# Differential attention with a dense eight-expert feed-forward: the q/k RMS norm cut into 512-column pieces, and the guard of the first expert weights set earlier

## The reference, cut to what matters

```
q, k, v = x @ wq.T, x @ wk.T, x @ wv.T              # 8 heads of 256
q1, q2  = rms_norm(first half of q), rms_norm(second half)   # halves of 128; k1, k2 likewise
y       = softmax(causal q1 k1) v - lambda * softmax(causal q2 k2) v
x1      = layernorm(x + 0.2 * (y @ wo.T))
w       = softmax over the top 2 of 8 gate logits x1 @ gate, scattered to 8 columns
out     = sum over all experts e of ((silu(x1 @ wi_0[e]) * (x1 @ wi_1[e])) * w[e]) @ wo[e]
result  = layernorm(x1 + out)
```

## Time and profile before

| | |
|---|---|
| runs shown | 9087.93 and 9921.32 us, median 9504.62 |
| the profiled execution, its own time | 9131.31 us |
| its span (core 2, the slowest) | 9129.8 us |
| spans of the eight cores | 9017.3 to 9129.8 us |
| PE busy, DVE busy, ACT busy | 7343.8 (80%), 1951.4 (21%), 2306.1 (25%) us |
| attention stage with projections | 0 to about 2707 us |
| output projection, layer norm, gate | to about 3237 us |
| experts | from 3244.6 us to the end |

### The profile page before, as it was taken

One profiled execution on the slowest core, in us unless ns is written; L12 is line 12 of the kernel. 1 busy time (PEld: TensorE's weight loads), 2 busy tenths in 40 slices (PEclk: granted clock), 3 DMA queues, 4 the chain that ended last, 5 costly groups with the idle time before them and its releaser, 6 DMA issues.

```text
span 9129.8 us, 78951 instructions; the slowest of 8 cores (9017.3 to 9129.8 us)
## 1 busy us (share of the span) xinstructions
PE 7343.8 (80%) x32250; PEld 3269.1 (36%) x32866; DVE 1951.4 (21%) x2548; ACT 2306.1 (25%) x2553; POOL 924.2 (10%) x822
## 2 busy tenths in 40 slices
PE   4546646646649189999999999969999999999996
PEld 2223213313314034444444444424444444444342
DVE  1222221222222511111111111131111111111113
ACT  3565565575560120110110100111001001011011
POOL 0000000000000011111111111101111111111110
PEclk8767767767769589999999999989999999999888
DMA  4001001101103067787787777757777778767664
GB/s 61 5 10 14 10 5 14 14 0 14 14 10 93 0 65 70 72 76 70 70 79 70 70 75 74 70 79 70 76 72 74 72 69 81 69 67 72 63 62 69
DMA packets 1663572, 483.60 MB, mean 53 GB/s; under 512 B 1589097, under 2 KB 1655017, under 8 KB 1661170
## 3 DMA queue, kind: packets, MB, share of 16 engines
q0 software_dynamic: 1655712, 444.71, 49.2%
q1 hardware_dynamic: 7506, 33.80, 1.0%
HBM read 906.34 MB, written 16.78 MB: 101 GB/s over the span
## 4 chain that ended last, share of the span: by engine, by line
PE 70%; ACT 11%; DMA 7%; issue 6%; DVE 5%; another core or an unknown queue 1%; DVEq 0%; POOL 0%; ACTq 0%; SPq 0%; POOLq 0%
PE PB L994 15%; PE P L931 10%; PE PB L925 10%; PE P L925 10%; PE PB L931 10%; DMA WOS<-wom 5%; PE PB L284 4%; ACT ATT L496 4%; PE PB L514 3%; ACT L496 3%; PE PB L609 2%; PE P L508 2%; PE PB L318 1%; PE PB L451 1%; DMA WI1S<-wi 1%
## 5 line engine op out<-in xcount | busy, mean ns | idle before, releaser
L994 PE MATMUL PB<-H,WOS 128*128 128x512 bf16 x8030 | 1850.9, 389 | 181.5 <-DVE H L964 88.3
L947 ACT ACT_TABLE_LOAD x256 | 328.4, 1283 | 4885.5 <-PE PB L931 3382.1
L994 PEld LDWEIGHTS PB<-H,WOS 128*128 128x128 bf16 x8192 | 804.2, 100 | 1228.3 <-issue 382.7
L451 PE MATMUL PB<-QT,KT 128*128 128x512 bf16 (+3 forms) x640 | 299.0, 486 | 865.9 <-ACT ATT L496 739.6
L925 PE MATMUL PB<-X1T,WI0S 128*128 128x512 bf16 x4014 | 919.8, 385 | 13.4 <-DMA WI1S<-wi 8.7
L931 PE MATMUL P<-X1T,WI1S 128*128 128x512 bf16 x4014 | 919.5, 385 | 4.7
L925 PE MATMUL P<-X1T,WI0S 128*128 128x512 bf16 x4013 | 917.9, 385 | 5.8 <-DMA WI1S<-wi 1.2
L931 PE MATMUL PB<-X1T,WI1S 128*128 128x512 bf16 x4012 | 915.9, 384 | 4.7
L496 ACT ACT_TABLE_LOAD x640 | 821.1, 1283 | 291.3 <-PE PB L451 223.6
L911 POOL DMA_DIRECT2D WI0S<-wi x256 | 293.1, 1145 | 3305.9 <-PE PB L931 1643.7
L1009 DVE TENSOR_TENSOR ACC<-ACC,PB 128x512 f32<-128x512 f32 x448 | 308.1, 688 | 1407.9 <-PE PB L994 1407.9
(11 more groups left out here) (125 smaller groups left out, 4241.1 us busy)
## 6 DMA issues: line engine op xcount, KB each, us to landing
WI0S<-wi POOLq DMA_DIRECT2D x256, 512.0 KB, 6.4
WI1S<-wi POOLq DMA_DIRECT2D x256, 512.0 KB, 8.3
WOS<-wom POOLq DMA_DIRECT2D x256, 512.0 KB, 6.4
OXF<-xt SPq DMA_DIRECT2D x16, 1024.0 KB, 6.1
outT<-OUTS SPq DMA_DIRECT2D x32, 512.0 KB, 2.6
XT<-xt POOLq DMA_DIRECT2D x16, 512.0 KB, 29.1
WS<-wqT POOLq DMA_DIRECT2D x8, 1024.0 KB, 9.7
WS<-wkT POOLq DMA_DIRECT2D x8, 1024.0 KB, 9.6
```

The lines of the kernel that those rows point to most:

```text
L451: _t.out = PT.inc(t.matmul(PB[bn][:, qs:512], KT[:, m * T + kt * 128: m * T + (kt + 1) * 128], QT[:, m * T + qb * 512 + qs: m * T + (qb + ...
L947: i = PS.inc(s.activation(SILU[:, c * 512:(c + 1) * 512], h0p[par][c][1], AF.Silu))
L994: mm = t.matmul(PB[bn][:], WOS[slot][:, mt * 128:(mt + 1) * 128], H[:, mt * TCH + c * 512: mt * TCH + (c + 1) * 512], start=(mt == 0), sto ...
```

## The change: what it does

Two things, and the moves in SBUF that they need.

**The norm section.** q and k are handled one after the other by the same code (`side` 0 and 1). VectorE squares 2048 columns of the one side into `SQ`, which now holds only one side. Then for each of four pieces of 512 columns: one matmul with the ones into `P2b` or `P2c` in turn, `Ln` and `Exp` on that bank, and the product on VectorE, which frees the bank. Each of these is a block of its own. `SQ` moves out from under `ATT`, so the wait for the readers of `ATT` goes.

**The guard.** The first loads of the expert weights wait for TensorE's last step before the layer norm (`attn_guard`) in place of its last step of the gate stage. `LOGIT` and `CWTOK` move to places that no expert weight slot covers.

```diff
-    SQ = al("SQ", [128, 2 * T], BF16, offset=C_OFF + 24576)
+    SQ = al("SQ", [128, T], BF16, offset=C_OFF + 61440)
...
-    LOGIT = al("LOGIT", [8, T], F32, offset=C_OFF + 32768)
-    CWTOK = al("CWTOK", [128, TT * E], F32, offset=C_OFF + 40960)
+    LOGIT = al("LOGIT", [8, T], F32, offset=C_OFF + 24576)
+    CWTOK = al("CWTOK", [128, TT * E], F32, offset=C_OFF + 60416)
...
             for m in range(2):
-                    for kt8 in range(8):
-                        wt(v, "v", att_cons[kt8])
-                    v.tensor_mul(SQ[:, 0:T], QT[:, m * T:(m + 1) * T], QT[:, m * T:(m + 1) * T])
-                    _vq.out = PV.inc(v.tensor_mul(SQ[:, T:2 * T], KT[:, m * T:(m + 1) * T],
-                                                  KT[:, m * T:(m + 1) * T]))
...
+                for side in range(2):
+                    buf = QT if side == 0 else KT
+                    def _vsq(v, m=m, side=side, buf=buf):
+                        if side == 0:
+                            for dep in proj_done:
+                                wt(v, "v", dep)
+                        wt(v, "v", (PT, sq_cons[0]))
+                        _vsq.out = PV.inc(v.tensor_mul(SQ[:], buf[:, m * T:(m + 1) * T],
+                                                       buf[:, m * T:(m + 1) * T]))
+                    VS(_vsq)
+                    sqv = _vsq.out
                     for c in range(4):
-                        mm = t.matmul(P2[:, c * 512:(c + 1) * 512], ONESB[:],
-                                      SQ[:, c * 512:(c + 1) * 512], start=True, stop=True)
...
+                        pb_name = "P2b" if c % 2 == 0 else "P2c"
+                        psl = P2[:, 512:1024] if c % 2 == 0 else P2[:, 1024:1536]
+                        def _t(t, c=c, sqv=sqv, pb_name=pb_name, psl=psl):
+                            wt(t, "t", (PV, sqv))
+                            wait_banks(t, [pb_name])
+                            _t.out = PT.inc(t.matmul(psl, ONESB[:],
+                                                     SQ[:, c * 512:(c + 1) * 512],
+                                                     start=True, stop=True))
+                        TS(_t)
+                        mmv = _t.out
+                        def _s(s, side=side, mmv=mmv, psl=psl):
+                            wt(s, "s", (PT, mmv))
+                            i = PS.inc(s.activation(psl, psl, AF.Ln, scale=1.0 / HALF,
+                                                    bias=CST[:, 0:1]))
+                            wt(s, "s", (PS, i))
+                            b2 = CST[:, 2:3] if side == 0 else CST[:, 3:4]
+                            _s.out = PS.inc(s.activation(psl, psl, AF.Exp, scale=-0.5, bias=b2))
+                        SS(_s)
+                        rv = _s.out
+                        def _v(v, m=m, c=c, buf=buf, rv=rv, psl=psl):
+                            wt(v, "v", (PS, rv))
+                            _v.out = PV.inc(v.tensor_tensor(
+                                buf[:, m * T + c * 512: m * T + (c + 1) * 512],
+                                buf[:, m * T + c * 512: m * T + (c + 1) * 512], psl, ALU.mult))
+                        VS(_v)
+                        rel_banks([pb_name], (PV, _v.out))
+                    if side == 0:
+                        q1n_val = _v.out
+                    else:
+                        k1n_val = _v.out
+                    sq_cons[0] = mmv
...
+        attn_guard = (PT, PT.n)
...
-    gate_guard = (PT, PT.n)
+    gate_guard = attn_guard
```

More of the change, by code:

```diff
@@ L358, in build @@
[L358 to L363, removed]
-                    for c in range(4):
-                        mm = t.matmul(P2[:, c * 512:(c + 1) * 512], ONESB[:],
-                                      SQ[:, c * 512:(c + 1) * 512], start=True, stop=True)
-                    _t.out = PT.inc(mm)
-                TS(_t)
-                ssq_val = _t.out
@@ L371, in _s @@
[L371 to L407, removed]
@@ L408, in build @@
-                VS(_v)
-                k1n_val = _v.out
-                rel_banks(p2_dep_all, (PV, k1n_val))
+                for side in range(2):
[9 more added lines that the diff above has]
+                    sqv = _vsq.out
+                    for c in range(4):
+                        pb_name = "P2b" if c % 2 == 0 else "P2c"
[29 more added lines that the diff above has]
+                    sq_cons[0] = mmv
```

## The result

The changed kernel took 9219.95 us in the median of 11 runs (9189.42 to 10123.68), against 9914.03 us of 10 runs for the one before (9087.93 to 10108.18). The ratio is **1.0128, 95% interval [1.0105, 1.0151]**: slower by 1.3%. The forecast was 9200 us, 0.95% more, told as no change within 2%. The time lies in the range of 9145 to 9290, but the loss is clear of noise and a third larger than said. The mean core went from 9038.5 us (23 dies, in the runs of the kernel before that were made together with the first experiments) to 9161.9 us (18 dies), 123 us more, where the sum had 87.

What follows compares the result with a forecast made beforehand. Norm sections were taken to lie on the path with their whole length, engines handing work to and fro. 94.6 less 7.6 gave 87 us more: 9218 from the profiled run, 9175 from the lower; 9200 was taken, range 9145 to 9290.

Steps and rivals of the forecast that it cites:

- the sum: Whole kernel: 94.6 us more from the norm sections less 7.6 us from the guard, 87 us more.
- Norm sections: Attention's 16 norm sections: eight table loads in place of two outweigh the overlap; 94.6 us more over 8 heads.
- The guard: Seam before the experts: earlier weight loads remove TensorE's DMA wait; 7.6 us less.
- the last clause of the forecast: Experts' stretch: nothing counted for any change in its length; a change there would prove the forecast wrong.
- The call: Whole kernel: 9200 us, 0.95% more, told as no change within 2%, with 0.90 chance of landing within 2%.
- The pieces that don't overlap: Rival 1, norm sections: a piece takes 4.32 us in place of 2.73, 153 us more, 9371 us; chance 0.05.
- No reload: Rival 2, norm sections: only a side's first piece loads tables; 119 us less, 9099 us, 0.4% faster; chance 0.04.
- What ACT_TABLE_LOAD costs: Norm's 96 added loads: page's 1.38 us draining each, 132 us more, 9350 us; extra over 1 us each, chance 0.03.

Runs made afterwards that it cites:

- guard alone: Early guard with the new places of LOGIT and CWTOK, in the kernel before with its norm section unchanged; ratio to before 0.9986.
- the norm alone: The changed kernel with the old guard for the expert weights, norm section in pieces; two runs of 9224.97 and 9239.39 us.
- ScalarE's padding: The kernel before with 370 idle one-element copies on ScalarE in the first 70 us; mean core 9049.5 us against 9048.8.
- the shorter stream: Against the kernel with one table load a side and a row of queries, each row's score matmuls in one TensorE block; two dies, 8466.0 and 8478.3 us.

## Why the prediction was wrong, and where it was right

**Norm sections: right in mechanism and size.** Said were 27.61 us for a half 1 and 27.40 for the first half 0; measured are 27.49 and 27.30 (157.51 to 184.81 on core 4). Pieces were to follow after 2.73 us and do. From the first score matmul to the last, core 4 went from 2526.4 to 2616.2 us, 89.8 more; the 15 sections between them were to bring 94.6 - 6.2 = 88.4.

**The guard: right in mechanism and size.** 7.6 us were said, from the one core of the earlier trace rows, where core 4 had 13.55. From the last score matmul to the first expert product the guard takes away 9.2 us (after against before), 8.6 (guard alone against before) and 7.2 (after against the norm alone).

**The step that failed** is the last clause of the forecast, that the experts' stretch counts nothing. Between the profiles, from before's cores 4 to 7 to all cores after, the mean span grows by 119.5 us (9039.2 to 9158.7). Of this 3.2 us lie ahead of the first score matmul and 88.6 between the first and the last, 9.2 are given back up to the first expert product, and 36.9 lie in the experts. The first three make 82.6 us, where the sum had 87; the fourth was missing, not mis-sized. Over the eight cores that stretch is 5727 us after, and it was 5688 over the six cores of before whose clock was at 0.98. It needs nothing of what the change computes: 40 idle matmuls alone make the stretch 43 us longer in the kernel before. That the changed kernel has its longer stretch for the same reason is inferred from the same landing times and waits; no run has the norm in pieces with before's stream on TensorE. Why a stream does this stays open.

**The call.** With 87 us I had called the outcome no change, by a bound of 2%. That step fails too: the interval of the ratio is 0.23% to either side here, so even the sum as it stood was a loss that a measurement shows. Also, 9200 mixed two bases: the profiled execution of before (9131.3) had its two longest cores at clocks of 0.878 and 0.879 where the others had 0.882 to 0.889, and the runs of before that followed at the usual clock took 9058.75 to 9116.82 us. From 9088, the sum alone gives 9175; the good agreement of 9200 with 9220 is partly luck: a base some 25 us too high stood in for part of the 39 us that were left out.

**The rivals.** The pieces that don't overlap were built (4.32 us a piece, 37.2 us a section) and are not what the change does. No reload (one load a side) was built too, and gives what it was said to, 122.6 us less than the changed kernel for 119; the changed kernel reloads in every block. The Trainium skill's page "ScalarE: Activation LUTs", section "What ACT_TABLE_LOAD costs", gives about 1.38 us of draining beside a load of 1.283, for every switch to a different set, and the prediction priced every load with it. The loads here stand 0.02 us behind the operation before them (2704.85 + 0.66 to 2705.53), and six fewer shorten the first section from 27.30 to 19.66 us, 1.27 each: no draining between blocks that use the same functions.

## What to carry to other kernels

Before cutting a chain into pieces, look whether each piece brings a fixed cost on the engine that will set the pace: here 1.28 us of table load for 1.3 us of work. If each block loads the tables, put many activations into one block; in this kernel that is worth 6%, and the cut of the norm, with its pieces in one block, 33 us of the attention stage. And where a load has 7 us of cover and takes 6.4, a change elsewhere can move the time by 0.3 to 0.4% without any work of its own: compare with a padded copy of the old kernel before explaining such a rest.

## What the runs showed that was not expected

The landing of the `WOS` loads has two values, and which one it is goes with TensorE's stream. The three kernels whose TensorE stream is that of before have the short one, 6.4 to 6.5 us on every core: before, the guard alone, ScalarE's padding, with `WOS` waits of 70.7, 77.1 and 78.8 us. All ten others have 6.6 us or more on every core, and waits of 91 to 105 us (means over the cores with a clock of 0.98 in the experts).

These are fewer cases than they seem. Five of the ten have the norm in pieces on TensorE, four the same 40 matmuls (three at the start, one at the end), and one the shorter stream. The short value was seen with a single stream, so the runs can't tell its length from anything else in it. How a stream does this (where program, weights and descriptors come to lie in memory would be one way) was not tried and stays open, as does which stream would bring the short value back.

In nearly every kernel one core of a pair waits 15 to 45 us longer for `WOS` than the other (115.7 and 86.6 us for cores 4 and 5 after). It is not always the same one, and how far apart the two start does not decide by how much: cores 4 and 5 before start 7.7 us apart and differ by 18 us, cores 0 and 1 after start 1.7 us apart and differ by 37.
